# A graph-attention aggregation kernel: the sum over eight slot columns moves from VectorE to TensorE

## The chip, the cores and the metric

The program runs on one core of one Trainium2 chip. The metric is the device time of the whole program in microseconds (us), lower is better. Before the change it took 10117.94 us, the median of three runs (10090.75 to 10120.89).

## The reference, cut to what matters

A node table of 6250 rows and 256 columns goes through four layers, each added to what came before: a graph attention (8 heads of 32), a small four-expert network gated by a second attention (4 heads of 4), a graph attention (4 heads of 64), and an eight-expert network. The change touches the first and the third:

```python
e = e_left[src] + e_right[dst]
e = jnp.where(e >= 0, e, NEG_SLOPE * e)
e_max = segment_max(e, dst, num_segments=N)
e_exp = jnp.exp(e - e_max[dst])
denom = segment_sum(e_exp, dst, num_segments=N)
alpha = e_exp / (denom[dst] + EPS)
out = segment_sum(Wh[src] * alpha[:, :, None], dst, num_segments=N)
```

For each of 6250 nodes, then, the rows of all its neighbours (206250 edges with both directions and the loops) are fetched, weighed by a softmax over the neighbours, and added up. All is float32.

## The kernel before, in words

The program is a sequence of blocks. In order: a sort of the edges by node, a ranking of the nodes by degree with dense work beside it, the first large aggregation, a ranking, a small aggregation with the four small experts beside it, a ranking, the last large aggregation, a dense stage, and the experts. `aggregate` is called twice, for the first large aggregation (8 heads of 32, rows of 272 words, a sort of the next lists beside it) and for the last (4 heads of 64, rows of 264 words, nothing beside it). In the trace they lie from 1002 to 3682 us and from 6250 to 8757 us. In both, 256 columns of result per node are made.

The nodes are ranked by degree and cut into 49 tiles of 128, one node to a partition, degrees rising. A node's neighbours are slots along the free dimension, gathered by GpSimd, one indirect DMA for one slot of all 128 nodes (L914), into a ring of 96 slots (`Stream.gpsimd`). Eight slots are a unit; a tile has three to eight of them and here fits one chunk (`nk` is 1, `ng` its slots). The two aggregations each gather 1728 slots. GpSimd waits on `taken` before it fills a ring entry of 16 slots again.

For each tile (`tile(t)` on VectorE, written out 49 times in the program with a loop over chunks and one over units inside):

- ScalarE, in `lay` (L1138 to L1146), copies the score columns of the gathered slots to `el`, as soon as the tile's last slot is in (`ready`), one tile ahead of VectorE, and then counts `laid`.
- VectorE makes the scores (L1055 to L1067), ScalarE the exponentials into `prob` in PSUM (L1155).
- VectorE weighs the tile's last unit into `wide` in SBUF (`weigh`, L1042), and then for each other unit (L1075 to L1080) weighs it into `part` in PSUM and adds `part` to `wide`. Both hold 2048 columns, eight slots of 256. `taken` frees the unit's ring space.
- The end of the chunk is L1081 to L1095: the sum of the exponentials (`dsum`), the old `den` and `acc` times their scale, then the eight slots of `wide` halved to four, two and one (L1087, L1089, L1091), and `acc` plus that (L1095).
- In the first aggregation VectorE then does its share of the sort (`beside.vector`, L177 to L197): ten or eleven steps a tile in tiles 0 to 16, three or four in tiles 17 to 48. Steps "turn" and "back" are transposes on TensorE (L217, L220), copied from PSUM by ScalarE (L234, L236). TensorE does nothing else in this block.
- The end of the tile is L1100 to L1108: `den` is inverted and `res` made as `acc` times `den`; ScalarE stores it (L1127).

All waits are on semaphores that count up, against values worked out in registers of each engine from the tile's sizes (`sizes_of`, L1006). Each engine runs its own program in the order in which it is written; nothing reorders it.

## Time and profile before

| What | Value |
|---|---|
| Median of three runs | 10117.94 us (10090.75 to 10120.89) |
| Span of the profiled execution | 10110.4 us; its own time is not listed apart from the three runs |
| VectorE busy | 5594.3 us (55%), 8828 instructions |
| GpSimd busy | 5337.1 us (53%) |
| TensorE matmul busy | 2288.8 us (23%) |
| ScalarE busy | 1093.7 us (11%) |
| Gathers of L914, 4320 in three aggregations | 4275.8 us, 990 ns each |
| Weighing into `part`, L1042, x420 | 964.4 us, 2296 ns each |
| Adding `part` to `wide`, L1080, x420 | 960.4 us, 2287 ns each |

The busy shares are averages over a dozen stages. The page's chain of waits names only the very end of the program, so what bounds an aggregation has to be read from the waits and the timeline inside its own stretch. "issue" in a row is idle time for which the profile shows no wait; names ending in q are an engine's instruction sequencer.

### The profile page before, as it was taken

How to read it: one execution, taken by the hardware profiler on the slowest of the kernel's cores; microseconds unless marked ns; L12 is line 12 of the kernel's file. 1: busy time of each engine (PE TensorE's matmuls, PEld its weight loads, DVE VectorE, ACT ScalarE, POOL GpSimd, SP SyncE). 2: the span in 40 equal slices, each digit the busy share in tenths (PEclk: the TensorE clock that was granted, in tenths of full speed). 3: DMA queues.
4: the chain of work that ended last, by engine and by line, in shares of the span. 5: the costliest groups of instructions: out<-in, count | busy, mean ns of one | idle time of the engine just before them, and what ended most of it. 6: DMA issues, size and time to landing. Idle time of an engine off the chain costs nothing. (4 is left out here: it accounts for less than half of the span.)

```text
span 10110.4 us, 54577 instructions
## 1 busy us (share of the span) xinstructions
PE 2288.8 (23%) x9111; PEld 1752.0 (17%) x9112; DVE 5594.3 (55%) x8828; ACT 1093.7 (11%) x2533; POOL 5337.1 (53%) x5411
## 2 busy tenths in 40 slices
PE   2112000000000002146555512000000000129995
PEld 1111000000000001135444411000000000116663
DVE  8764588788777677523333275455656556421111
ACT  1101000000000001112222201000000000002221
POOL 0025656666676654455555345776666777542221
PEclk7555555555555555578777755555555555559997
DMA  4051333433333353411111162433333333620004
GB/s 142 22 159 50 97 82 87 122 99 98 101 101 98 102 113 74 122 23 33 29 28 28 30 172 89 109 100 92 101 98 101 106 99 99 129 97 30 30 30 117
DMA packets 458121, 869.43 MB, mean 86 GB/s; under 512 B 175134, under 2 KB 294860, under 8 KB 448192
## 3 DMA queue, kind: packets, MB, share of 16 engines
q0 software_dynamic: 239536, 575.99, 23.0%
q1 hardware_dynamic: 167648, 182.04, 6.2%
q10 hardware_dynamic: 50788, 110.02, 3.3%
q14 instruction: 129, 1.06, 0.0%
q8 instruction: 20, 0.33, 0.0%
HBM read 693.35 MB, written 180.71 MB: 86 GB/s over the span
## 5 line engine op out<-in xcount | busy, mean ns | idle before, releaser
L914 POOL DMA_INDIRECT agg_ring<-table,agg_idx x4320 | 4275.8, 990 | 2329.8 <-issue 1323.4
L1042 DVE TENSOR_TENSOR agg_part<-agg_ring,agg_prob 128x2048 f32 x420 | 964.4, 2296 | 631.8 <-issue 556.2
L1080 DVE TENSOR_TENSOR agg_wide<-agg_wide,agg_part 128x2048 f32<-128x2048 f32 x420 | 960.4, 2287 | 14.4
L1786 PE MATMUL dense_tp<-all_ident,dense_xn 128*128 128x128 f32 x100 | 23.9, 425 | 2570.3 <-issue 2543.7
L1408 PE MATMUL agg_hp<-agg_xt,agg_w 128*128 128x256 f32 x1600 | 446.4, 439 | 579.4 <-ACT agg_ht L1378 340.3
L2208 DVE TENSOR_TENSOR experts_h<-experts_sg,experts_hp 128x682 f32<-128x682 f32 x106 | 91.8, 866 | 779.7 <-ACT experts_sg L2191 779.7
L2158 PE MATMUL experts_hp<-mixture_w,experts_xt 128*128 x1696 | 518.2, 458 | 0.6 <-ACT experts_xt L2187 0.6
L1408 PEld LDWEIGHTS agg_hp<-agg_xt,agg_w 128*128 128x128 f32 x1600 | 352.4, 224 | 663.8 <-ACT agg_ht L1378 360.4
L1786 PEld LDWEIGHTS dense_tp<-all_ident,dense_xn 128*128 128x128 f32 x100 | 20.3, 228 | 2571.9 <-issue 2544.5
L2129 POOL DMA_INDIRECT yc<-experts_ysb,experts_list x105 | 103.7, 987 | 685.2 <-DVE experts_ysb L2217 685.2
L1422 PE MATMUL agg_yp<-agg_w,agg_ht 128*128 128x256 f32 x1600 | 405.3, 411 | 231.0 <-remote 174.5
L1422 PEld LDWEIGHTS agg_yp<-agg_w,agg_ht 128*128 128x128 f32 x1600 | 330.4, 208 | 297.1 <-issue 246.9
L1042 DVE TENSOR_TENSOR agg_wide<-agg_ring,agg_prob 128x2048 f32 x98 | 224.2, 2288 | 275.0 <-issue 198.8
L488 POOL IOTA rank_thresholds<- 128x50 int32 x3 | 0.5, 170 | 686.4 <-POOLq L75 686.4
L2158 PEld LDWEIGHTS experts_hp<-mixture_w,experts_xt 128*128 128x128 f32 x1696 | 314.4, 190 | 174.6 <-issue 30.0
L217 PE MATMUL agg_words_turned<-all_ident,last_sort_words 128*128 128x128 f32 x48 | 10.9, 416 | 1454.1 <-issue 1454.1
L2179 PE MATMUL experts_yp<-mixture_w,experts_ht 128*128 x1260 | 309.4, 387 | 0.0
L1155 ACT ACTIVATE agg_prob<-agg_score 128x648 f32<-128x648 f32 (+1 forms) x98 | 56.7, 579 | 2332.1 <-issue 1387.9
L1055 DVE TENSOR_TENSOR agg_score<-agg_el,agg_er 128x640 f32<-128x640 f32 (+1 forms) x98 | 64.6, 659 | 410.0 <-issue 372.4
L514 POOL DMA_INDIRECT rank_start_g<-starts,rank_node_i x147 | 143.3, 975 | 225.9 <-DVE rank_degt L625 182.0
L217 PEld LDWEIGHTS agg_words_turned<-all_ident,last_sort_words 128*128 128x128 f32 x48 | 8.8, 216 | 1456.4 <-issue 1456.0
L522 POOL DMA_INDIRECT rank_wide<-copies,rank_widx x147 | 148.9, 1013 | 195.6 <-DVE rank_widx L679 154.8
(421 smaller groups left out, 6520.8 us busy)
## 6 DMA issues: line engine op xcount, KB each, us to landing
agg_ring<-table,agg_idx POOLq DMA_INDIRECT x4320
y<-agg_ysb ACTq DMA_DIRECT2D x25, 1024.0 KB
rank_y<-y SPq DMA_DIRECT2D x10, 2560.0 KB
rank_x<-x SPq DMA_DIRECT2D x30, 640.0 KB
copies<-first_sort_words SPq DMA_DIRECT2D x16, 1024.0 KB
copies<-last_sort_words ACTq DMA_DIRECT2D x16, 1024.0 KB
x<-rank_x SPq DMA_DIRECT2D x20, 640.0 KB
agg<-agg_res ACTq DMA_DIRECT2D x98, 128.0 KB
```

Of the source, the lines that this page charges most:

```text
L514: pool.indirect_dma_start(out=start_g[:, t:t + 1], out_offset=None, in_=starts.rearrange("(n a) -> n a", a=1), in_offset=bass.IndirectOffs ...
L522: pool.indirect_dma_start(out=wide[g % 2][:, u * ROW:(u + 1) * ROW], out_offset=None, in_=copies.rearrange("c (r w) -> (c r) w", w=ROW), i ...
L914: pool.indirect_dma_start(out=self.ring[:, to:to + self.RW], out_offset=None, in_=self.table, in_offset=bass.IndirectOffsetOnAxis(ap=index ...
L1042: return dve.tensor_tensor(to[:, :].rearrange("p (j h c) -> p j h c", j=UNIT, h=H), ring[:, ds(st.at(at_u), UNIT * RW)].rearrange("p (j w) ...
L1055: dve.tensor_tensor(sc3, el3, er[:, H:2 * H].unsqueeze(1).to_broadcast([P, SC // H, H]), ALU.add).then_inc(added, 1)
L1080: dve.tensor_tensor(wide[:, :], wide[:, :], part[:, :], ALU.add).then_inc(widened, 1)
L1408: mm = pe.matmul(self.hp[:, h:h + 2 * P], self.w1[:, at:at + P], xt3[:, :, k * P:(k + 1) * P], start=(k == 0), stop=(k == 1))
L1422: mm = pe.matmul(y, self.ht[:, n * 2 * P + u * P:n * 2 * P + (u + 1) * P], self.w2[:, n * D:(n + 1) * D], start=(c == 0), stop=(c == 3))
L2129: pool.indirect_dma_start(out=yc, in_=ysb[t % B][:, :], in_offset=None, out_offset=bass.IndirectOffsetOnAxis(ap=lst[:, t * 4 + 1:t * 4 + 2 ...
L2158: mm = pe.matmul(hp3[:, c, 0:HC], xt[:, kc * P:(kc + 1) * P], rhs, start=(kc == 0), stop=(kc == 1))
L2179: mm = pe.matmul(yp[:, 0:D], ht[0:m, j * P:(j + 1) * P], w2[0:m, ds(e * W2 + j * D, D)], start=(j == 0), stop=(j == HJ - 1))
L2208: dve.tensor_tensor(h[:, :].rearrange("p (c n) -> p c n", c=2), sg[:, :].rearrange("p (c n) -> p c n", c=2), hp3[:, 2:4, 0:HC], ALU.mult). ...
```

## The change

In both large aggregations TensorE adds up the eight slots of `wide`. After a chunk's last unit has been added (`widened`), it multiplies the identity with each of the eight 256-column pieces of `wide`, all accumulating in `part[:, 0:256]` in PSUM (`folded`). VectorE no longer halves `wide` three times and has no `summed`. The folded sum is added to `acc` either before the weighing of the next chunk or tile (`merged`), while ScalarE makes the exponentials, or, for the result, into `res`, which is then multiplied by `den` in a second instruction (`completed`). TensorE now needs the tile's sizes in its registers. The sizes are stored as six 16-bit words instead of five 32-bit ones, one of them split in two.

```diff
 def aggregate(...):
-        sizes = s.sb("sizes", [1, 5 * (NT + 1)], I32)
+        sizes = s.sb("sizes", [1, LOAD * (NT + 1)], mybir.dt.uint16)
+        bits, split = s.sb("bits", [1, 2 * (NT + 1)], I32), s.sem("split")
...
-            ng, nk, c0, k0, missing = nc.values_load_multi_w_load_instructions(sizes[0:1, ds(t * 5, 5)], ...)[1]
+            ng, nk, c_high, c_low, k0, missing = nc.values_load_multi_w_load_instructions(
+                sizes[0:1, ds(t * LOAD, LOAD)], ...)[1]
...
             @block.vector
+                dve.memset(part[:, 0:CW], 0.0).then_inc(const, 1)
...
+                dve.sem_inc(folded, 1)
...
                 def tile(t):
                     ng, nk, c0, k0, _ = sizes_of(dve, t)
+                    kn = dve.snap(k0 + nk)
                     with dve.Fori(0, nk) as k:
...
                         dve.tensor_tensor(sc3, sc3, mn[:, :].unsqueeze(1).to_broadcast([P, SC // H, H]), ALU.subtract).then_inc(scored, 1)
+                        dve.wait_ge(folded, kk)
+                        dve.tensor_tensor(acc[:, :], acc[:, :], part[:, 0:CW], ALU.add).then_inc(merged, 1)
                         dve.wait_ge(probs, kk)
...
                         dve.wait_ge(tail, kk)
+                        dve.wait_ge(merged, kk)
...
                         dve.tensor_tensor(acc3, acc3, prob_scale.unsqueeze(2).to_broadcast([P, H, C]), ALU.mult).then_inc(scaled, 1)
-                        dve.wait_ge(widened, n1)
-                        dve.tensor_tensor(wide[:, 0:4 * CW], wide[:, 0:4 * CW], wide[:, 4 * CW:8 * CW], ALU.add).then_inc(quartered, 1)
-                        dve.wait_ge(quartered, kk)
-                        dve.tensor_tensor(wide[:, 0:2 * CW], wide[:, 0:2 * CW], wide[:, 2 * CW:4 * CW], ALU.add).then_inc(halved, 1)
-                        dve.wait_ge(halved, kk)
-                        dve.tensor_tensor(summed[:, :], wide[:, 0:CW], wide[:, CW:2 * CW], ALU.add).then_inc(folded, 1)
+                        dve.tensor_tensor(den[:, :], den[:, :], dsum[:, :], ALU.add).then_inc(dens, 1)
                         dve.wait_ge(scaled, kk)
-                        dve.tensor_tensor(den[:, :], den[:, :], dsum[:, :], ALU.add).then_inc(dens, 1)
-                        dve.wait_ge(folded, kk)
-                        dve.tensor_tensor(acc[:, :], acc[:, :], summed[:, :], ALU.add).then_inc(combined, 1)
...
-                    dve.tensor_tensor(res[:, :].rearrange("p (h c) -> p h c", h=H), acc3,
+                    dve.wait_ge(folded, kn + 1)
+                    dve.tensor_tensor(res[:, :], acc[:, :], part[:, 0:CW], ALU.add).then_inc(completed, 1)
+                    dve.wait_ge(completed, t + 1)
+                    res3 = res[:, :].rearrange("p (h c) -> p h c", h=H)
+                    dve.tensor_tensor(res3, res3,
                                       den[:, :].unsqueeze(2).to_broadcast([P, H, C]), ALU.mult).then_inc(tile_done, 1)
...
             @block.tensor
+                def fold(t):
+                    ng, nk, c0, _, _ = sizes_of(pe, t)
+                    with pe.Fori(0, nk) as k:
+                        gg = c0 + k * ng
+                        n1 = pe.snap((gg + ng) // UNIT + cfg.RU)
+                        pe.wait_ge(widened, n1)
+                        for j in range(UNIT):
+                            mm = pe.matmul(part[:, 0:CW], S["ident"][:, :], wide[:, j * CW:(j + 1) * CW], start=j == 0, stop=j == UNIT - 1)
+                        mm.then_inc(folded, 1)
...
+                if beside.parts:
+                    for t in range(NT):
+                        fold(t)
+                        beside.tensor(pe, t)
+                else:
+                    with pe.Fori(0, NT) as t:
+                        fold(t)
```

VectorE, end of a chunk in the first aggregation (a tile with three sort steps behind it). Before:

```order
L1081 TENSOR_REDUCE agg_dsum<-agg_prob 128x8
L1083 TENSOR_TENSOR agg_den<-agg_den,agg_prob 128x8 [waits agg0_totalled]
L1085 TENSOR_TENSOR agg_acc<-agg_acc,agg_prob 128x256 [waits agg0_shrunk]
L1086 REGISTER_ALU
L1087 TENSOR_TENSOR agg_wide<-agg_wide 128x1024 [waits agg0_widened]
L1089 TENSOR_TENSOR agg_wide<-agg_wide 128x512 [waits agg0_quartered]
L1091 TENSOR_TENSOR agg_summed<-agg_wide 128x256 [waits agg0_halved]
L1093 TENSOR_TENSOR agg_den<-agg_den,agg_dsum 128x8 [waits agg0_scaled]
L1095 TENSOR_TENSOR agg_acc<-agg_acc,agg_summed 128x256 [waits agg0_folded]
L1049 REGISTER_ALU [waits agg0_combined,agg0_dens]
L1049 COMPARE_AND_BRANCH
L197 TENSOR_TENSOR last_sort_words<-last_sort_words 128x2x64x4 [waits last_sort_words_compared]
```

And with the change:

```order
L1097 TENSOR_REDUCE agg_dsum<-agg_prob 128x8
L1099 TENSOR_TENSOR agg_den<-agg_den,agg_prob 128x8 [waits agg0_totalled]
L1101 TENSOR_TENSOR agg_acc<-agg_acc,agg_prob 128x256 [waits agg0_shrunk]
L1102 TENSOR_TENSOR agg_den<-agg_den,agg_dsum 128x8
L1062 REGISTER_ALU [waits agg0_scaled,agg0_dens]
L1062 COMPARE_AND_BRANCH
L197 TENSOR_TENSOR last_sort_words<-last_sort_words 128x2x64x4 [waits last_sort_words_compared]
```

Five instructions fewer lie between the last unit and the sort (or, in the last aggregation, the end of the tile). At the end of the same tile one instruction of before, L1108, has become two, with a wait for TensorE (`folded`) and the register instruction of that wait ahead of them:

```order
L1107 MEMSET agg_m 128x8
L1109 TENSOR_SCALAR agg_den<-agg_den 128x8 [waits agg0_reset]
L1111 RECIPROCAL agg_den<-agg_den 128x8 [waits agg0_floored]
L1115 ISA [waits agg0_out_stored,agg0_inverted]
L1116 TENSOR_TENSOR agg_res<-agg_acc,agg_part 128x256 [waits agg0_folded]
L1119 TENSOR_TENSOR agg_res<-agg_res,agg_den 128x256 [waits agg0_completed]
```

TensorE, sort transposes of tiles 13 (L217, a turn) and 14 (L220, the way back). Before:

```order
L217 MATMUL agg_words_turned<-all_ident,next_sort_words 128x128 [waits next_sort_words_copied,next_sort_words_compared]
L217 MATMUL agg_words_turned<-all_ident,next_sort_words 128x128 x7
L220 MATMUL agg_words_turned<-all_ident,next_sort_words 128x128 [waits next_sort_words_copied,next_sort_words_compared]
L220 MATMUL agg_words_turned<-all_ident,next_sort_words 128x128 x7
L217 MATMUL agg_words_turned<-all_ident,next_sort_words 128x128 [waits next_sort_words_copied,next_sort_words_compared]
```

And with the change:

```order
L217 MATMUL agg_words_turned<-all_ident,next_sort_words 128x128 [waits next_sort_words_copied,next_sort_words_compared]
L217 MATMUL agg_words_turned<-all_ident,next_sort_words 128x128 x7
L1011 TENSOR_LOAD agg_sizes
L1129 UNCONDITIONAL_BRANCH
L1129 ISA
L1134 MATMUL agg_part<-agg_wide,all_ident 128x256 [waits agg0_widened]
L1134 MATMUL agg_part<-agg_wide,all_ident 128x256 x7
L1129 REGISTER_ALU
L1129 COMPARE_AND_BRANCH
L220 MATMUL agg_words_turned<-all_ident,next_sort_words 128x128 [waits next_sort_words_copied,next_sort_words_compared]
L220 MATMUL agg_words_turned<-all_ident,next_sort_words 128x128 x7
L1011 TENSOR_LOAD agg_sizes
```

The way back of tile 14 was next in line on TensorE once VectorE had compared; now the fold of tile 14, which waits for that tile's last unit, stands between the two.

## Rows read from the trace of the kernel before

**Rows 1.** busy time by stretch: from, to, us, each engine busy (instructions), PEclk, DMA share, GB/s

```profile
1002.00:3682.00 2680.00, 49.97 (x208) 39.87 (x208) 2008.21 (x2144) 178.63 (x457) 1720.85 (x1729) 0.50 0.37 97
6250.00:8757.00 2507.00, 0.00 (x0) 0.00 (x0) 1440.70 (x1445) 116.18 (x414) 1767.46 (x1763) 0.50 0.38 97
```

**Rows 2.** groups of VectorE, 1000 to 3680 us: shapes, count, busy us, mean ns, idle before

```profile
L1080 DVE TENSOR_TENSOR agg_wide<-agg_wide,agg_part 128x2048 f32<-128x2048 f32 x210 | 480.2, 2287 | 7.2
...
L1087 DVE TENSOR_TENSOR agg_wide<-agg_wide 128x1024 f32<-128x1024 f32 x49 | 59.9, 1222 | 0.0
...
L1108 DVE TENSOR_TENSOR agg_res<-agg_acc,agg_den 128x256 f32<-128x256 f32 x49 | 21.5, 439 | 14.7 <-DVE agg_den L1104 6.0 <-remote 3.8 <-issue 3.6
```

**Rows 3.** why GpSimd's gathers (L914) waited, 1000 to 3670 us (us, times)

```profile
  DVE agg_part L1042: 384.7, 35
```

**Rows 4.** the same, 6300 to 8770 us

```profile
  DVE agg_part L1042: 146.2, 28
```

**Rows 5.** timeline, scores laid out (ACT) and taken up (DVE): start us, us, [idle before]

```profile
1086.92 0.74 ACT L1146 ACTIVATE agg_el<-agg_negs 128x640 f32 x1 [1.09 <-issue]
...
1132.52 0.82 DVE L1055 TENSOR_TENSOR agg_score<-agg_el,agg_er 128x640 f32<-128x640 f32 x1 [1.03 <-issue]
...
3387.46 0.74 ACT L1146 ACTIVATE agg_el<-agg_negs 128x640 f32 x1 [1.09 <-issue]
...
3390.80 0.83 DVE L1055 TENSOR_TENSOR agg_score<-agg_el,agg_er 128x640 f32<-128x640 f32 x1 [1.02 <-issue]
...
3617.12 0.83 DVE L1055 TENSOR_TENSOR agg_score<-agg_el,agg_er 128x640 f32<-128x640 f32 x1 [27.63 <-ACT agg_el L1146]
...
8488.40 0.49 DVE L1055 TENSOR_TENSOR agg_score<-agg_el,agg_er 128x320 f32<-128x320 f32 x1 [7.12 <-issue]
```

**Rows 6.** timeline of VectorE, end of one tile of the first aggregation

```profile
2119.16 0.82 DVE L1081 TENSOR_REDUCE agg_dsum<-agg_prob 128x8 f32<-128x640 f32 x1
...
2120.21 0.42 DVE L1085 TENSOR_TENSOR agg_acc<-agg_acc,agg_prob 128x256 f32<-128x256 f32 x1
...
2122.53 0.43 DVE L1091 TENSOR_TENSOR agg_summed<-agg_wide 128x256 f32<-128x256 f32 x1
2122.87 0.22 DVE L1093 TENSOR_TENSOR agg_den<-agg_den,agg_dsum 128x8 f32<-128x8 f32 x1
...
2123.77 0.69 DVE L197 TENSOR_TENSOR last_sort_words<-last_sort_words 128x512 f32<-128x512 f32 x1 [0.35 <-DVE agg_acc L1095]
```

**Rows 7.** timeline of VectorE, end of one tile of the last aggregation

```profile
7497.41 2.29 DVE L1080 TENSOR_TENSOR agg_wide<-agg_wide,agg_part 128x2048 f32<-128x2048 f32 x1
...
7504.88 0.43 DVE L1108 TENSOR_TENSOR agg_res<-agg_acc,agg_den 128x256 f32<-128x256 f32 x1 [0.49 <-issue]
7509.78 0.49 DVE L1055 TENSOR_TENSOR agg_score<-agg_el,agg_er 128x320 f32<-128x320 f32 x1 [4.47 <-issue]
```

**Rows 8.** timeline of TensorE: 128x256 matmuls after work, after idling, one by one

```profile
4297.90 1.89 PE L1408 MATMUL agg_hp<-agg_xt,agg_w 128*128 128x256 f32 x8
4309.23 3.78 PE L1408 MATMUL agg_hp<-agg_xt,agg_w 128*128 128x256 f32 x8 [9.44 <-issue]
...
4315.35 0.38 PE L1422 MATMUL agg_yp<-agg_w,agg_ht 128*128 128x256 f32 x1 [1.92 <-issue]
```

**Rows 9.** timeline of TensorE and ScalarE, one turn of the sort

```profile
1384.40 1.97 PE L217 MATMUL agg_words_turned<-all_ident,next_sort_words 128*128 128x128 f32 x8 [439.17 <-DVE next_sort_words L190]
...
1386.40 0.60 ACT L234 ACTIVATE next_sort_words<-agg_words_turned 128x512 f32<-128x512 f32 x1 [0.26 <-issue]
```

**Rows 10.** timeline of VectorE, first weighing of a tile behind the exponential

```profile
3620.78 0.83 DVE L1067 TENSOR_TENSOR agg_score<-agg_score,agg_mn 128x640 f32<-128x640 f32 x1
3623.13 2.29 DVE L1042 TENSOR_TENSOR agg_wide<-agg_ring,agg_prob 128x2048 f32 x1 [1.52 <-ACT agg_prob L1155]
```

**Rows 11.** register instructions at L1042, first then last aggregation: ns min/median/max

```profile
L1042 DVEq FUSED_REGOPS  x567: 4/168/1425, 1062.6 to 3656.4; - x189
...
L1042 DVEq FUSED_REGOPS  x567: 4/698/1414, 6365.6 to 8742.1; - x189
```

35 lines of the change are left out of this document (20 added, 15 removed).

## The prediction

> **What bounds the kernel now.** The page's chain names only the end of the program, so I read the two aggregations by stretch. [rows 1] is the first view: over 2680 us and 2507 us VectorE is busy 75% and 57%, GpSimd 64% and 71%, TensorE hardly or not at all, with its clock at 0.50. Neither engine fills its stretch, so the next view is who waits for whom. GpSimd's gathers wait for VectorE to free ring space for 384.7 us in the first aggregation [rows 3] and 146.2 us in the last [rows 4]. Third comes the other direction. VectorE begins a tile at L1055; what it needs from the gathers is there when L1146 ends. I looked at all 98 such pairs. In the first aggregation the scores of tile 1 lie ready 45 us before they are taken up, those of tile 45 still 2.6 us (3387.46 + 0.74 to 3390.80), and only the last tile, 48, waits for them, 27.6 us [rows 5]. So VectorE sets the pace of tiles 1 to 47, with the reserve shrinking as the tiles grow. In the last aggregation tiles 0 to 7 begin as soon as their scores are ready (gathers bind), tiles 8 to 37 have 6 to 35 us of reserve (VectorE binds), and after tile 37 GpSimd gathers with hardly a wait until the last tile, so that its own pace counts; tile 45 begins late again [rows 5]. So about 30 of 49 tiles there are paced by VectorE.
>
> **First aggregation, end of a chunk.** From L1081 to the sort's first step the row times give 2123.77 - 2119.16 = 4.61 us [rows 6]. With the change the three halvings and the last addition go. L1085 still ends 1.47 us after L1081 began; the addition to `den` follows as closely as it does behind L1091 (0.34 us after its start), lasts 0.16 to 0.22 us, and the loop's branch costs 0.35 us as now: 1.95 us. That takes off 2.66 us.
>
> **End of the tile.** L1108 (0.44 us, [rows 2]) becomes two instructions of that size, 0.42 us plus 0.03 between: +0.45 us. The one more register instruction is 0.05 us, or 0.7 us where such instructions are slow [rows 11]; some seven tiles of this stretch are so (their unit loops are longer than those of tiles with as many units), +5 us. Net 2.2 us a tile. `part` lies in PSUM. A 2048-column addition that reads PSUM takes 2287 ns, a 1024-column one in SBUF 1222 ns [rows 2]; the difference is 1065 ns, 1.04 ns for each further column, and between that SBUF one and a 512-column step of the sort in SBUF (0.69 us, [rows 6]) it is also 1.04 ns a column. So I charge nothing for PSUM. The Trainium skill, "VectorE: DVE Perf Modes", in the section on the errata, gives a PSUM source 62 cycles more of fixed time than an SBUF one. By it the 98 additions into `res` would cost some 6 us more, an estimate from that page; the trace does not bear it out.
>
> **The merge** into `acc` (0.42 us) stands between L1067 and the wait for the exponentials. VectorE idles 1.52 us there [rows 10], 0.71 us of it for ScalarE: it is covered, at nothing; uncovered it would be 0.42 us x 98 = 41 us.
>
> **The fold.** Eight 128x256 float32 matmuls took 1.89 us behind other work and 3.78 us after 9 us of idling [rows 8]. TensorE idles for some 30 us before nearly every fold, and [rows 1] has its clock at 0.50 throughout, 1.2 GHz; I take 3.8 us, plus 0.1 us for semaphores each way: ready 4.0 us after the last unit. The Trainium skill, "TensorE: Matmul & The Clock Gate", in the section on what is happening, calls the throttled clock the default and says that activity releases it; the rows agree, with 1.89 and 3.78 us. Were the clock at its upper level here, the fold would take 1.9 us and the last aggregation save about 1.5 us a tile more, 45 us in all. In the first aggregation VectorE has at least 5 us of sort between, so nobody waits for the fold.
>
> **Transposes behind the fold.** In tiles 10, 14 and 16 (and 37) the sort's first step is a turn or a way back that TensorE now does before the tile's end, and then behind its fold. There VectorE would be ready 1.95 us after L1081 starts, but fold (3.9), eight transposes (1.97) and the last copy (0.26 + 0.60) [rows 9] end at 6.7 us: 4.8 us lost in each, and about 8 us in tile 37, with sixteen transposes. Together 22 us. In the other sixteen, sort work of VectorE lies ahead of the transpose.
>
> **Sum of the first.** 48 tiles x 2.2 = 106 us; minus 22 for the transposes and 5 for slow register instructions; minus 4 because tiles 44 and 45 have too little reserve to run 7 us ahead of the gathers [rows 5]; minus 2 for tile 47, whose gain is lost in the last tile's wait: 73 us.
>
> **Sum of the last.** Here nothing lies between chunk and tile end. Before, L1108 ends at 7505.31, 5.6 us after the last L1080 (7497.41 + 2.29 = 7499.70) [rows 7]. With the change the fold is ready at +4.0; then 0.42, 0.03 and 0.42: +4.9. VectorE arrives at about +3.2, so it stands 0.8 us for TensorE. Gain 0.7 us (0.3 where register instructions are quick). x 30 tiles = 21 us, and 0.7 for the last tile. The other 18 are paced by the gathers and gain nothing. `lay` on ScalarE and the loads of six sizes have the reserve above them; the constants at the start cost about 1 us twice.
>
> 73 + 22 - 2 = 93 us. The profiled span is 10110.4 us, 7.5 us below the median of the runs; 10110.4 - 93 = 10017 as a span, and 10025 as a median. By the bounds: without the losses to transposes and reserve 120 us; with a PSUM read that costs 6 us in all after all, half the merge uncovered and a fold of 4.5 us, 93 - 6 - 20 - 15 = 52 us. So the forecast's own range is 9998 to 10066.
>
> **Rivals.**
> *TensorE issues slowly, and VectorE stands for it (slower).* New code on TensorE once ran one matmul at a time, 1.92 us idle before one of 0.38 us [rows 8]. A fold at 2.3 us a matmul is 18 us. In the last aggregation each VectorE-paced tile stands 14 us longer, 30 x 14 = 420 us; in the first the sort hides 8 to 16 us of it, another 6 us a tile, 290 us: some 10700 us. It decides from a fold of 4.0 + 93/30 = 7 us. Against it: all 20 turns and ways back in the first aggregation, also written out once each, ran without gaps [rows 9]. 10%.
> *The gathers bind (no change).* GpSimd's 384.7 us of waits are unevenly spread, and the reserve of VectorE falls to 2.6 us at tile 45. If the ring of 96 slots passes on only a part, and the fold eats the last aggregation's 21 us, 25 us are left: 10093 us. 12%.
> *Register instructions change their pace (either sign).* At L1042 they last 168 ns in the first and 698 ns in the last aggregation, the same 567 of them [rows 11]: same code, and the trace does not say what makes them slow. The change moves all code. If the slow kind spreads over the first, up to 567 x 0.53 = 300 us more, some 10320 us; a third of it eats the gain. 7%. If it leaves the last, VectorE gains as much, but GpSimd has only 146 us of waits to give, of which 20 are spent above: 9900 us. 8%.
>
> **How the numbers follow.** The forecast has 63%, the rivals 10, 12, 7 and 8%. What can be told from no change is 0.3%, 30 us: 10088 to 10148. Faster: 63 + 8 + 2 (a mild form of the second rival) = 73%. Slower: the first and the bad half of the third, 17%. The same: 10%. The range goes from 9900 (the good half of the third) to 10125 (the second rival with a margin); what lies above is left out, some 17%.
>
> **What would show it.** L1087 to L1095 gone; the start of the sort about 2.0 us after the start of the `dsum` reduction; folds of 3.8 us at a clock of 0.50; no wait for the fold in the first aggregation but one of 5 us for ScalarE's copies in tiles 10, 14 and 16; in the last a wait of 0.8 us on TensorE ahead of the addition into `res`; the first aggregation 70 us and the last 20 us shorter, with GpSimd's waits down by about as much. Wrong it would be if GpSimd's waits fell and the stretches did not (gathers bind), if folds took over 7 us, or if the median of the register instructions moved in either stretch.

## The result, and the profile after

The changed kernel takes 10385.79 us (median of five runs, 10383.11 to 10399.96) where the kernel before takes 10117.94: a ratio of 1.0266, 95% interval 1.025 to 1.0283. The forecast was 10025, faster; the time lies far above the range. The profiled execution spans 10381.2 us, 270.8 more than before. A sum of the stretches, from a stretch's first gather to its last result, says where: the first aggregation takes 2886.7 us and not 2664.3 (+222.4), the last 2456.6 and not 2434.0 (+22.6), the small aggregation and the rankings between them 25.0 more, the rest 0.8. The code between the two is unchanged, and over the traces of the experiments from chips like this one the small aggregation takes 1490 to 1561 us (1518 before, 1537 after), so the 25.0 us are not shown to come from the change.

The page of the profile after: each engine's busy time, then TensorE's busy share and its granted clock in 40 slices, in tenths.

```profile
PE 2858.1 (28%) x10679; PEld 2188.5 (21%) x10680; DVE 5411.3 (52%) x8638; ACT 1093.1 (11%) x2533; POOL 5254.5 (51%) x5411
...
PE   2212011111111111225654432011111111129995
...
PEclk9555555555555555557877765555555555559997
```

VectorE is busy 183 us less, as the change meant it to be, and the program is longer. The same two stretches as [rows 1], in the same columns:

```profile
1002.00:3905.00 2903.00, 327.75 (x992) 252.27 (x992) 1915.26 (x2049) 178.24 (x457) 1708.11 (x1728) 0.55 0.35 90
...
6555.00:9027.00 2472.00, 293.98 (x784) 224.46 (x784) 1343.37 (x1316) 111.97 (x405) 1662.57 (x1729) 0.55 0.38 98
```

x784 for 49 folds is 16 records a fold, not eight. I come back to that.

VectorE's groups in the last aggregation, in the columns of [rows 2]. What is new is the idle time ahead of L1116, the addition that takes the fold into `res`; what has gone is idle time ahead of the weighing (L1054, L1042 before) and of the scores (L1068, L1055 before).

```profile
L1054 DVE TENSOR_TENSOR agg_part<-agg_ring,agg_prob 128x2048 f32 x210 | 482.3, 2297 | 109.3 <-issue 51.4 <-DVE agg_wide L1096 44.8 <-DVE agg_wide L1054 13.1
...
L1068 DVE TENSOR_TENSOR agg_score<-agg_el,agg_er 128x320 f32<-128x320 f32 x49 | 24.3, 497 | 136.9 <-issue 136.9
...
L1116 DVE TENSOR_TENSOR agg_res<-agg_acc,agg_part 128x256 f32<-128x256 f32 x49 | 20.7, 422 | 776.1 <-remote 583.8 <-issue 188.0 <-PE agg_part L1134 4.3
```

The kernel before, same groups in its last aggregation:

```profile
L1042 DVE TENSOR_TENSOR agg_part<-agg_ring,agg_prob 128x2048 f32 x210 | 482.2, 2296 | 491.5 <-issue 480.9 <-DVE agg_wide L1080 5.4 <-DVE agg_wide L1042 5.2
...
L1055 DVE TENSOR_TENSOR agg_score<-agg_el,agg_er 128x320 f32<-128x320 f32 x49 | 24.1, 492 | 293.1 <-issue 283.1 <-ACT agg_el L1146 6.5 <-DMA agg<-agg_res 3.5
```

So the fold costs 776 us of standing, 15.8 us a tile, and the stretch is only 23 us longer, because some 640 us of other idle time went (382 ahead of the weighing into `part`, 104 ahead of that into `wide`, and 156 ahead of the scores), and 97 us of additions. With the first two go slow register instructions: at L1054 they have the quick pace in both stretches now, against [rows 11] (first, then last aggregation).

```profile
L1054 DVEq FUSED_REGOPS  x567: 46/211/306, 1063.4 to 3881.7; - x189
...
L1054 DVEq FUSED_REGOPS  x567: 46/211/701, 6613.7 to 9010.6; - x189
```

One tile end of the last aggregation (TensorE, then VectorE), the place of [rows 7]:

```profile
7443.09 5.35 PE L1134 MATMUL agg_part<-agg_wide,all_ident 128*128 128x256 f32 x16 [42.89 <-DVE agg_wide L1096]
...
7444.89 0.18 DVE L1111 RECIPROCAL agg_den<-agg_den 128x4 f32<-128x4 f32 x1
7455.73 0.42 DVE L1116 TENSOR_TENSOR agg_res<-agg_acc,agg_part 128x256 f32<-128x256 f32 x1 [10.66 <-remote]
```

TensorE begins 0.05 us after the last addition to `wide`, all 16 records are issued within 5.0 us, and VectorE gets the sum 12.6 us after the first. "remote" means that the profile has no instruction that ends when the wait does: as recorded, the matmuls ended long before. Over the 49 tiles that time is 10 to 21 us, 19 in the middle, with one exception, the last tile, when no gather is under way any more and no further TensorE instruction comes behind the fold. There it is 6.2 us:

```profile
9014.98 6.16 PE L1134 MATMUL agg_part<-agg_wide,all_ident 128*128 128x256 f32 x16 [82.17 <-DVE agg_wide L1096]
...
9021.18 0.42 DVE L1116 TENSOR_TENSOR agg_res<-agg_acc,agg_part 128x256 f32<-128x256 f32 x1 [4.32 <-PE agg_part L1134]
```

In the first aggregation the stands for the fold are 170 us in 26 tiles, but the larger part is elsewhere. TensorE and then ScalarE, a turn of the sort behind a fold:

```profile
3065.85 6.01 PE L1134 MATMUL agg_part<-agg_wide,all_ident 128*128 128x256 f32 x16 [44.40 <-issue]
3071.70 1.04 PE L217 MATMUL agg_words_turned<-all_ident,last_sort_words 128*128 128x128 f32 x8
3096.11 1.12 PE L217 MATMUL agg_words_turned<-all_ident,last_sort_words 128*128 128x128 f32 x4 [23.38 <-issue]
...
3095.46 0.60 ACT L234 ACTIVATE last_sort_words<-agg_words_turned 128x512 f32<-128x512 f32 x1 [43.40 <-remote]
3104.56 0.60 ACT L234 ACTIVATE last_sort_words<-agg_words_turned 128x512 f32<-128x512 f32 x1 [8.50 <-remote]
```

The x8 are two groups of four transposes. A free TensorE gives the first group to ScalarE 1.2 us after its start; here it comes 23.8 us after it, and the second group 32.9. VectorE's idle time ahead of its sort steps (L184, L190, L197) rises from 179 to 407 us, GpSimd's waits for VectorE from 384.7 [rows 3] to 634.6 us, those of [rows 4] from 146.2 to 252.7.

### The profile page after: what moved, and what is told of

Same layout as the page of the kernel before. It is cut to its first block and busy times, and to the rows that moved or that the text cites. A ratio compares the mean times of both kernels' runs of the same rounds, so it can differ in the third digit from the quotient of the medians.

```text
span 10381.2 us, 58165 instructions
## 1 busy us (share of the span) xinstructions
PE 2858.1 (28%) x10679; PEld 2188.5 (21%) x10680; DVE 5411.3 (52%) x8638; ACT 1093.1 (11%) x2533; POOL 5254.5 (51%) x5411
## 5 line engine op out<-in xcount | busy, mean ns | idle before, releaser
L914 POOL DMA_INDIRECT agg_ring<-table,agg_idx x4320 | 4192.4, 970 | 2679.7 <-issue 1298.0
L1134 PE MATMUL agg_part<-agg_wide,all_ident 128*128 128x256 f32 x1568 | 583.2, 552 | 4637.0 <-DVE agg_wide L1096 2651.0
L1134 PEld LDWEIGHTS agg_part<-agg_wide,all_ident 128*128 128x128 f32 x1568 | 446.0, 292 | 4773.7 <-DVE agg_wide L1096 2672.5
L1054 DVE TENSOR_TENSOR agg_part<-agg_ring,agg_prob 128x2048 f32 x420 | 964.6, 2297 | 219.7 <-DVE agg_wide L1096 104.2
L1116 DVE TENSOR_TENSOR agg_res<-agg_acc,agg_part 128x256 f32<-128x256 f32 x98 | 41.3, 422 | 950.7 <-remote 729.4
L1054 DVE TENSOR_TENSOR agg_wide<-agg_ring,agg_prob 128x2048 f32 x98 | 224.2, 2288 | 153.0 <-ACT agg_prob L1183 83.6
L190 DVE TENSOR_TENSOR last_sort_words<-last_sort_words 128x1024 f32<-128x1024 f32 x176 | 209.3, 1230 | 91.7 <-ACT last_sort_words L236 64.2
L506 POOL DMA_INDIRECT rank_row<-words,rank_qi x150 | 152.0, 1013 | 193.0 <-DVE rank_junk L593 89.9
```

What stands on the lines that cost most here:

```text
L190: dve.tensor_tensor(b[:, :, half, :], a[:, :, 0, :], a[:, :, 1, :], op).then_inc(self.cmp_done, 1)
L506: pool.indirect_dma_start(out=row[i % 2][:, v * COARSE:(v + 1) * COARSE], out_offset=None, in_=rows, in_offset=bass.IndirectOffsetOnAxis(a ...
L914: pool.indirect_dma_start(out=self.ring[:, to:to + self.RW], out_offset=None, in_=self.table, in_offset=bass.IndirectOffsetOnAxis(ap=index ...
L1054: return dve.tensor_tensor(to[:, :].rearrange("p (j h c) -> p j h c", j=UNIT, h=H), ring[:, ds(st.at(at_u), UNIT * RW)].rearrange("p (j w) ...
L1134: mm = pe.matmul(part[:, 0:CW], S["ident"][:, :], wide[:, j * CW:(j + 1) * CW], start=j == 0, stop=j == UNIT - 1)
```

## The experiments

The changed kernel's aggregations are the base of all edits. The experiments ran on seven chips, and these are of two kinds. On four, like the one above, the kernel before takes 10089 to 10122 us; on three it takes 9118 to 9128 us. Each comparison of times below is with the kernel before on the same chip; traces of the kernel before exist from the first chip alone. e1, e2, e6, f3 and g3 ran once each, so their totals carry no interval.

The theory at the start: beside the gathers each matmul of a fold arrives late. Its rivals: a fixed hold of the last signal, and a burst after which TensorE is slow.

**How many matmuls (e1_count, e6_count_again).** VectorE halves `wide` 0, 0, 1, 2 or 3 times, TensorE folds the rest, the first class twice over.

```diff
+                    count = (16, 8, 4, 2, 1)[t % 5]
...
+                        for again in range(2 if count == 16 else 1):
+                            n = min(count, UNIT)
+                            for j in range(n):
```

> The changed kernel, but the number of 128x256 matmuls in a fold goes round with the tile: 16 (the eight done twice), 8, 4, 2, 1; VectorE halves `wide` zero, zero, one, two or three times before, so the result stays right. In the changed kernel the eight leave TensorE's records within 6 us but are taken up by VectorE 12 to 21 us after the first one's start (last aggregation). Theory 'each is slow beside the gathers' (about 1.2 us for each of the 16 records): in the last aggregation the time from a fold's first matmul to the addition into res is about 38, 19, 10, 5 and 2.5 us. Rival 'a fixed hold' (what is late is only the signal of the last one): about 19 us for every number. Rival 'a burst switches TensorE down' (slow only after some 3 us of unbroken work, when the granted clock steps): 2 and 1 matmuls arrive in under 2.5 us, 4 in 4 to 6, 8 in 19, 16 in much more than 30.

It ran on a chip where before takes 9119.42 us: 9139.59. From first matmul to the addition into `res`, in the last aggregation, in the middle: 9.7, 5.8, 3.8, 2.1 and 1.3 us. Nothing is late there, gathers or not, and all three theories were left without a case; so it went to another chip.

> e1_count once more, on another chip. On a chip where before takes some 10120 us (as in e5) and a fold of eight is taken up 12 to 21 us after its first matmul, the numbers 16, 8, 4, 2, 1 tell what the lateness is. 'Each matmul is late' (about 2.4 us for each of the eight): 38, 19, 10, 5, 2.5 us. 'A fixed hold of the last signal': 26, 19, 17, 15, 14 us. 'A burst of over some 3 us switches TensorE down': 16 and 8 late, 4 at most 4 us, 2 and 1 at 2.1 and 1.3 us. On a chip where before takes 9119 us: 9.7, 6.0, 3.8, 2.1, 1.3 us, as in e1_count.

Before 10122.06, this 10571.3 us. In the same order now: 24 to 64 us for sixteen (43 in the middle), 9 to 19 us for eight (17), and 3.6 to 3.8 us for four, in all ten tiles. Two and one were there when VectorE came for them or within 2.4 us. Three tiles in a row, TensorE and VectorE:

```profile
8375.92 9.27 PE L1147 MATMUL agg_part<-agg_wide,all_ident 128*128 128x256 f32 x32 [54.28 <-issue]
...
8427.51 0.42 DVE L1125 TENSOR_TENSOR agg_res<-agg_acc,agg_part 128x256 f32<-128x256 f32 x1 [47.83 <-remote]
...
8463.11 6.58 PE L1147 MATMUL agg_part<-agg_wide,all_ident 128*128 128x256 f32 x16 [77.92 <-issue]
...
8481.46 0.42 DVE L1125 TENSOR_TENSOR agg_res<-agg_acc,agg_part 128x256 f32<-128x256 f32 x1 [17.54 <-issue]
...
8513.56 3.54 PE L1147 MATMUL agg_part<-agg_wide,all_ident 128*128 128x256 f32 x8 [43.87 <-issue]
...
8517.14 0.42 DVE L1125 TENSOR_TENSOR agg_res<-agg_acc,agg_part 128x256 f32<-128x256 f32 x1 [2.63 <-issue]
```

Four matmuls leave x8 records of 3.54 us; eight leave x16. The lateness is neither the same for each matmul nor a fixed hold of the signal: four matmuls are on time, the excess for eight is some 12 us and for sixteen some 33. That kills the first two theories as they were stated.

**No gathers (e2_no_gathers).** Ten more folds behind the last tile of each aggregation, each after ten VectorE instructions on `wide`.

```diff
+                for i in range(10):
+                    pe.wait_ge(again, i + 1)
+                    for j in range(UNIT):
+                        mm = pe.matmul(part[:, CW:2 * CW], S["ident"][:, :], wide[:, j * CW:(j + 1) * CW], start=j == 0, stop=j == UNIT - 1)
+                    mm.then_inc(refolded, 1)
```

> The changed kernel with ten more folds of eight matmuls behind the last tile of each aggregation, each after ten VectorE instructions of about 2.3 us on `wide`, when no gather is under way; VectorE waits for each. Theory 'slow beside the gathers': each of these is there about 6 us after its first matmul, as the last tile's own (6.2 us). Rival 'a burst switches TensorE down': 12 to 20 us each, like the folds inside the aggregation, whatever the gathers do. Rival 'fixed hold by what follows on TensorE': between them. The rest of the kernel as the changed one; the total about 2 x 10 x (24 + 6) = 600 us more.

9645.59 us, before 9119.42: a chip without lateness, so it told nothing of the gathers' part; the added folds arrive after 5.2 to 6.8 us, the ordinary ones of the last aggregation after 5.1 to 6.8. It was not repeated on a chip of the other kind, so whether gathers must be under way for the lateness is open. What speaks for it is the last tile of the last aggregation, whose fold arrives after 6.1 to 6.5 us in all four traces of the change from chips with late folds.

**Nobody stands for the fold (e3_deferred, e7_deferred_again; e4_deferred_swapped, e8_swapped_again).** `wide`, `acc` and `den` alternate by tile, the sum has a PSUM bank of its own (the sort's transposes give up one), and VectorE takes it at the end of the next chunk; e4 and e8 also put the transposes ahead of the fold.

```diff
+                        dve.wait_ge(folded, kk1)
+                        dve.tensor_tensor(accs[:, ds(whose, CW)], accs[:, ds(whose, CW)], total, ALU.add).then_inc(merged, 1)
...
-                        fold(t)
-                        beside.tensor(pe, t)
+                        beside.tensor(pe, t)
+                        fold(t, wides[t % 2])
```

> TensorE's fold stays, but nobody stands for it: `wide`, `acc` and `den` alternate between two buffers by tile, the sum goes to a PSUM bank of its own, VectorE takes it into the tile's `acc` at the end of the next chunk (0.42 us) and makes the result then, ScalarE stores it one tile later. If the stand for the fold is the cause of the loss in the last aggregation (584 us there by the waits), the last aggregation is no longer than before the change (2434 us from first gather to last result, or some 20 to 60 us less), and what remains is the loss of the first, where turns of the sort stand behind the fold: some 150 to 250 us slower than before there, total 10150 to 10300 us. If something else costs the time (register instructions, the loads of sizes), the total stays near 10390.

> As e3_deferred, and TensorE does the tile's transposes of the sort before the tile's fold instead of behind it. If the turns were late only because they stood behind a slow fold, the first aggregation is as long as before the change or up to 100 us shorter (48 tiles x 2.2 us), total 9950 to 10100 us. If the fold leaves TensorE slow for tens of us, whatever the order, turns stay late and the total is near e3_deferred's.

Where before takes 9119.42 us: 9067.35 (ratio 0.9944, 0.9927 to 0.996) and 9054.92 (0.9931, 0.9915 to 0.9948).

> e3_deferred once more, on another chip. Where signals of TensorE are late (before 10120 us): nobody stands for the fold, so by the waits shown in the changed kernel the last aggregation loses 770 us of stands against it and is bound by the gathers again or by VectorE; total 10000 to 10200 us. Rival 'the sort's late turns are most of the loss': 10250 us and more. Where before takes 9119 us: 9067 us as in e3_deferred.

> e4_deferred_swapped once more, on another chip. Where signals of TensorE are late: if the turns of the sort are late only because they stand behind the fold, 100 to 200 us less than e7_deferred_again; if TensorE stays slow for tens of us after a fold, or turns are late by themselves, within 50 us of it. Where before takes 9119 us: 9055 us as in e4_deferred_swapped.

Where before takes 10122.06 us: 10450.6 (1.0335, 1.0311 to 1.0359), worse than the change itself, and 10165.12 (1.0048, 1.0033 to 1.0063). The time expected for e7, 10000 to 10200 us, missed, and its rival, that late turns are most of the loss, came out: nobody stands for the fold, and the first aggregation still takes 2945 us (2896 in the change on the same chip, e9), because the turns stand behind it. The order alone makes 270 us of that: in e8, which differs from e7 in nothing else, the same stretch takes 2675 us, VectorE idles 205 us ahead of sort steps and not 448, and the total is 285 us less, where 100 to 200 were expected. So on these chips late turns are the main loss of the first aggregation. The lateness passes: in e8 ScalarE's first copy of most turns comes 1.15 us after the turn begins. Not told apart in e7 and e8 is what the lost bank costs, with which each group of four transposes waits for the copy of the one before.

The stand itself cost the last aggregation next to nothing. It takes 2461 us in e7 and 2459 in e8, where nobody stands, and 2455 in e9 with 774 us of stands, on the same chip. Without the stands the register instructions at L1054 are slow again there, 690 ns in the middle in both.

**The change on each kind of chip (e5_after_again, e9_after_third, g1_after_fourth, h2_after_fifth).** No edit.

> The changed kernel itself, unedited, beside the kernel before on the chip of the experiments, where before takes 9119 us and not 10118. In the four experiments there a fold of eight arrives 5.4 to 6.8 us after its first matmul (last tile of the recorded profile: 6.2), with and without gathers. Theory 'the time depends on how late TensorE's signals arrive on a chip': here the addition into res in the last aggregation waits about 4 us and not 16, no turn of the sort is late, and the verdict turns: by the terms of the prediction with a fold of 6 us instead of 3.8, first aggregation 70 us shorter, last 0 to 40 us longer, total 9050 to 9120 us, ratio 0.992 to 1.000. Rival 'the change costs 2.7% on any chip': 9360 us.

> The changed kernel itself beside these on the same chip. 10380 us and a ratio of 1.025 where before takes 10120 us; where before takes 9119 us and a fold arrives 6 us after its first matmul, 9050 to 9120 us and a ratio of 0.992 to 1.000 (as expected for e5_after_again, which ran on a chip of the first kind).

> The changed kernel, unedited, once more. So far it ran only on chips where before takes 10120 us (ratio 1.025 and 1.027). Where before takes 9120 us: e2_no_gathers had the changed kernel's first aggregation in 2411 us and the last in 2196 us from first gather to last result, against 2400 and 2196 in e4_deferred_swapped at 9055 us in all; so 9055 to 9085 us, a ratio of 0.993 to 0.996. Where before takes 10120: 1.026 again.

> The changed kernel, unedited, on the same chip as h1_split. Where before takes 9120 us: from e2_no_gathers, whose time less its twenty extra folds (292 and 290 us, by the same stretches in e3_deferred) is 9062 us, 9055 to 9085 us, a ratio of 0.993 to 0.996. Where before takes 10120 us: 1.022 to 1.027 again.

The first three fell on chips of the first kind: 10371.6 against 10121.78 (1.0254, 1.024 to 1.0268), 10388.46 against 10122.06 (1.0272, 1.0246 to 1.0297), 10302.42 against 10097.05 (1.0216, 1.0192 to 1.0239). The last did not: 9067.64 us against 9118.5, a ratio of 0.9946, 0.9929 to 0.9962. There the change is faster, by 0.5%. Its stretches in the columns of [rows 1]:

```profile
975.00:3402.00 2427.00, 328.44 (x992) 253.39 (x992) 1917.08 (x2049) 175.05 (x457) 1724.08 (x1728) 0.55 0.42 107
...
5522.00:7732.00 2210.00, 290.21 (x784) 221.92 (x784) 1342.64 (x1315) 108.31 (x405) 1644.28 (x1728) 0.56 0.43 109
```

And what VectorE and GpSimd waited for there, in the last aggregation:

```profile
DVE agg_score L1068 <- ACT agg_el L1174: 441.0, 37, 47.3
DVE agg_res L1116 <- PE agg_part L1134: 199.4, 49, 4.8
...
POOL agg_ring L914 <- DVE agg_part L1054: 8.2, 9, 5.8
```

The same busy times to within 1.5% (ScalarE's within 3.5%), and from first gather to last result the first aggregation is 475 us shorter than in the changed kernel's first trace, the last 262. The fold costs 4.1 us of standing a tile, GpSimd waits for VectorE 8.2 us in all, and VectorE waits for scores of slots just gathered: here the gathers set the pace of the last aggregation.

**Short folds throughout (f1_half, g2_half_again; f2_half_deferred).** One halving stays on VectorE, TensorE folds four; f2 is this with nobody standing.

```diff
+                        dve.wait_ge(widened, n1)
+                        dve.tensor_tensor(wide[:, 0:4 * CW], wide[:, 0:4 * CW], wide[:, 4 * CW:8 * CW], ALU.add).then_inc(halved, 1)
...
-                        for j in range(UNIT):
+                        for j in range(UNIT // 2):
```

> The change with shorter folds: VectorE adds the two halves of `wide` once (1.22 us, right behind the unit loop) and TensorE folds four pieces, in about 3.8 us, as the folds of four in the runs before. If what loses time on a chip with late folds is TensorE's work beyond some 3.8 us in one go, the wait ahead of the addition into res falls from 16 to 3 us, no turn of the sort is late, first aggregation 30 to 50 us shorter than before the change, last within 40 us: total 10070 to 10140 us (where before takes 10120), 9060 to 9120 us (where before takes 9119). If every TensorE result is late beside VectorE's wait, 10300 us and more.

> Folds of four as in f1_half, and nobody stands for them (two buffers of `wide`, `acc`, `den`, result made one tile later, transposes ahead of the fold, as in e8_swapped_again). VectorE gives up 1.1 us of additions a tile against before in both aggregations. If bursts are the cause, 10030 to 10110 us where before takes 10120 (e8_swapped_again: 10165), so this one beats the kernel before; where before takes 9119 us, within 20 us of e4_deferred_swapped's 9055. If the deferral itself costs (more register instructions, of the slow kind), it stays near 10160.

> f1_half once more, for a chip with late folds. Where before takes 10120 us: burst theory 10070 to 10140 us, wait ahead of the addition into res 3 us, no late turns, first aggregation (first gather to last result) 2620 to 2670 us against 2664 before and 2887 in the changed kernel; rival 'every TensorE result is late there' 10300 and more. Where before takes 9128: 9147 as in f1_half.

Where before takes 9128.34 us: 9147.31 (1.0022, 1.0012 to 1.0031) and 9148.87 (1.0022, 1.0012 to 1.0032). Both missed: f1 lies 27 us above its range and f2 94 us above the 9055 that it should have been near; f2 was not run on the other kind. On such a chip the 1.22 us of the halving is paid in the first aggregation, which takes 2460 us in f1 and 2414 with the fold of eight in f3 on the same chip. Where before takes 10097.05: 10170.78 (1.0076, 1.0059 to 1.0093), above what I expected. The stand ahead of the addition into `res` is at most 3.0 us (108 us for 48 tiles) and the last aggregation 2436 us, as before the change, but the first takes 2741 us, and VectorE's idle time ahead of sort steps is still 279 us. As I read it, a turn right behind a fold of four is too much work again; no run tests that. And the slow register instructions of the last aggregation are back.

```profile
L1054 DVEq FUSED_REGOPS  x567: 3/697/1395, 6400.4 to 8776.9; - x189
```

**A pause in the fold (f3_pause, g3_pause_again).** In the last aggregation alone the fold is done four and four, and VectorE zeroes unused columns 6 or 12 times between.

```diff
+                            if j == UNIT // 2 - 1 and not beside.parts:
+                                mm.then_inc(halfway, 1)
+                                pe.wait_ge(go, pe.snap(k0 + k + 1))
```

> The change's fold of eight, in the last aggregation alone done as four and four, with a pause between: VectorE waits for the first four, then writes zeros into unused columns of `part` 6 or 12 times (0.95 us each, odd and even tiles), then lets TensorE go on; result unchanged. If the unbroken burst is the cause, on a chip with late folds each half arrives 3.8 us after its first matmul. If it is the volume (eight matmuls within some time), the second half arrives as late as in the changed kernel, 8 to 15 us after its own first matmul, above all behind the short pause. First aggregation as the changed kernel's (2890 us from first gather to last result).

> f3_pause once more, for a chip with late folds: burst theory, each half 3.8 us after its first matmul whatever the pause; volume rival, second half 8 to 15 us after its own first matmul behind the short pause (6 instructions) and less behind the long one (12). Where before takes 9128 us: 3.8 us in any case, as in f3_pause.

f3 (9355.08 us, before 9128.34): 3.8 us for each half. g3 (10450.02 us, before 10097.05): the first half is in VectorE's hands after at most 4.2 us in all 49 tiles; the second after at most 3.82 us in all 25 tiles with the long pause, and after 3.5 to 9.4 us (7.3 in the middle) with the short one, over 4 us in 16 of 24. Two tiles, the long pause and the short, TensorE and then VectorE:

```profile
8467.69 3.78 PE L1141 MATMUL agg_part<-agg_wide,all_ident 128*128 128x256 f32 x8 [39.11 <-issue]
8486.10 3.68 PE L1141 MATMUL agg_part<-agg_wide,all_ident 128*128 128x256 f32 x8 [14.62 <-issue]
8524.30 3.78 PE L1141 MATMUL agg_part<-agg_wide,all_ident 128*128 128x256 f32 x8 [34.53 <-issue]
8535.50 3.78 PE L1141 MATMUL agg_part<-agg_wide,all_ident 128*128 128x256 f32 x8 [7.42 <-issue]
...
8489.81 0.42 DVE L1123 TENSOR_TENSOR agg_res<-agg_acc,agg_part 128x256 f32<-128x256 f32 x1 [3.83 <-issue]
...
8544.91 0.42 DVE L1123 TENSOR_TENSOR agg_res<-agg_acc,agg_part 128x256 f32<-128x256 f32 x1 [9.52 <-remote]
```

So it is no matter of an unbroken run alone: behind the short pause the first half still counts in 16 of 24 tiles, behind the long one in none. Within these stretches that fits a limit on what TensorE has lately done, from which it recovers when left alone. It is not shown that TensorE's load alone decides, and the last section has a stretch that speaks against it.

**The fold cut in two, deferred (h1_split, h3_split_again).** e4 with the second four begun when the next tile's first unit is added. This is right as long as a tile is one chunk, as here.

```diff
+                            if j == UNIT // 2 and pause:
+                                pe.wait_ge(widened, n2)
```

> e8_swapped_again's kernel with the fold of eight cut in four and four: TensorE goes on with the second four when VectorE has added the first unit of the next tile's chunk (some 15 us after the first four began; this form is right where every tile is one chunk, as with these inputs). Burst theory: no part of the fold is late on any chip and no turn of the sort stands behind one. Where before takes 10120 us: 10080 to 10160 us (e8: 10165), and whether it beats before hangs on the register instructions of 0.7 us in the last aggregation, of which this form has some more. Where before takes 9120 us: 9055 us as e4_deferred_swapped, a ratio of 0.993.

> h1_split once more, for a chip with late folds. Where before takes 10120 us: burst theory 10080 to 10160 us, every half of a fold there within 4 us, no late turns; e8_swapped_again, whose fold is unbroken, took 10165. If it is no less than e8, the rest of the loss is VectorE's own (register instructions of 0.7 us), not TensorE's lateness. Where before takes 9120 us: 9052 us again.

9052.37 us against 9118.5 (0.993, 0.9913 to 0.9946), and 10110.93 against 10089.29 (1.002, 1.0007 to 1.0032). On the late chips that is 0.3% better than e8 by the ratios, whose intervals just do not meet, and the fold loses nothing that I can find: the first aggregation takes 2644.5 us against 2664.3 in the trace before (on another chip of the kind), and VectorE's idle time ahead of sort steps is 186 us against 179. What is left does not look like the fold. The last aggregation takes 2450.7 us against 2434.0. VectorE's idle time on "issue" there is 408 us ahead of the weighing into `part` (481 before), but 210 ahead of that into `wide` (140), 128 ahead of the product into `res` (15) and 55 ahead of taking in the fold, and its register instructions have the slow pace:

```profile
L1054 DVEq FUSED_REGOPS  x567: 2/691/1396, 6373.8 to 8764.0; - x189
```

This form is level with e4 where nothing is late and the best edit where folds are late, but there it does not beat the kernel before.

## Why the prediction was wrong

- **The step that failed is "The fold", and with it "Sum of the last" and "Transposes behind the fold".** It read [rows 8] as eight matmuls in 3.78 us. A row's x counts records, and a float32 matmul of this kernel leaves two (a transpose one): four matmuls are x8 in 3.54 us, eight are x16. Even with nothing late a fold takes 6.0 us in the middle, not 3.8. The page before could have told: the loops of L1408 issue 32 matmuls for each of 25 blocks, 800 in all, and it counts 1600.

```profile
L1408 PE MATMUL agg_hp<-agg_xt,agg_w 128*128 128x256 f32 x1600 | 446.4, 439 | 579.4 <-ACT agg_ht L1378 340.3
```

  The Trainium skill, "FP8 and Floating Point Precision", in the section on TensorE's precision, gives true float32 four passes through the array; the trace agrees, with two records of 0.44 us for each 256 columns, some 0.22 us four times.
- **On the chip of the result it then took 19 us in the middle, and VectorE stood 15.8 us a tile for it, not 0.8.** The forecast took a result to be there when its records end. The first aggregation before already had rows against that, and the "ran without gaps" of the first rival looked at records alone. The sixteen transposes of one turn lie within 3.38 us, and ScalarE, which copies four at a time, gets the third group 9.1 us after the start and the fourth 20.3 (TensorE, then those two copies of ScalarE). On a chip without lateness (h2) the four copies of such a run follow at 1.2, 2.0, 3.0 and 3.7 us.

```profile
3160.42 3.38 PE L217 MATMUL agg_words_turned<-all_ident,last_sort_words 128*128 128x128 f32 x16 [183.58 <-issue]
...
3169.49 0.60 ACT L234 ACTIVATE last_sort_words<-agg_words_turned 128x512 f32<-128x512 f32 x1 [6.47 <-remote]
3180.75 0.60 ACT L234 ACTIVATE last_sort_words<-agg_words_turned 128x512 f32<-128x512 f32 x1 [10.66 <-remote]
```

- **VectorE came for the fold some 2 us after its first matmul and not 3.2** (12.64 less 10.66 us in the tile shown above), at the quick pace of the register instructions. On a chip without lateness a fold of 6.0 us therefore costs 4.1 us of standing.
- **The sign stood larger in a stretch of which I read TensorE's rows alone [rows 8].** In the small aggregation, where TensorE works in long runs, ScalarE and VectorE waited for it without a recorded cause. From the kernel before (4255 to 5774 us), and then from the changed kernel on a chip without lateness (3940 to 5040 us):

```profile
ACT agg_ht L1378 <- remote: 504.0, 46, 32.2
...
DVE agg_ysb L1394 <- remote: 170.5, 15, 32.7
```

```profile
ACT agg_ht L1406 <- PE agg_hp L1436: 226.3, 106, 4.3
```

  The longest such wait is 32 us on the one and 4.3 us on the other, for the same matmuls. The stretch takes 1518 us on the first and 1084 on the second.
- **Rival "TensorE issues slowly, and VectorE stands for it" was the right outcome by the wrong mechanism.** It priced a fold at 18 us, as it came, and said 10700 us. The issue was in time, what came late was the result. And it charged the stand in full: it left out that VectorE's register instructions turn quick when VectorE stands, some 490 us of idle time in the last aggregation. Its 10% was too little.
- **Transposes:** 22 us for four tiles became 228 us more of idle time ahead of sort steps, 107 of it in those four tiles and 121 in others, whose transposes were called covered. They were taken as late by the fold's length; TensorE stays late after it.
- **What held:** the sort begins 1.85 us after L1097 (2115.70 against 2113.85; forecast 1.95). L1082 is hidden behind ScalarE's exponential, as forecast: idle time ahead of the first weighing falls from 120.4 to 102.3 us. `part` in PSUM costs the additions nothing: L1116 takes 422 ns and L1082 414, the SBUF additions L1091 and L1095 425 each. So the 62 cycles of the Trainium skill, "VectorE: DVE Perf Modes", section on the errata, are not borne out here. L1116 and L1119 are 0.42, 0.03 and 0.42 us.
- **Where results are not late the change gains 50.9 us,** just under the forecast's smallest gain, 52. That it comes so near is in part luck: the stand is 4.1 us and not 0.8, and goes unseen because the gathers set the pace of the last aggregation there (the second rival). That the first aggregation gives all of the gain follows from this but is not shown, since no trace of the kernel before was taken on such a chip.
- **Register instructions:** the last aggregation got the quick pace, which the third rival priced at 9900 us. It came with stands, so that it gave back and did not give.

## What to carry to other kernels

Before work is moved to an engine that idles, read how it behaves under load of that length, in whatever stretch of the trace has it: in these traces waits for it marked "remote" meant that its results came later than its records ended. Look for the sign in the stretch to be changed above all: the stage with TensorE's longest runs here shows no such wait (last section), the aggregation does. Check how many records one instruction leaves before a row's x is used as a count. Keep added work short and off the waits of others, put it behind what has a reader, and compare on more than one chip: here one change is 2.2 to 2.7% slower on some and 0.5% faster on others.

## What was not expected of the hardware

- **Chips differ by 10% for the same kernel**: 9118 to 9128 us on three, 10089 to 10122 us on four and on the first. The first aggregation of the changed kernel takes 2411 us on the one kind, 2852 to 2906 on the other. Two things mark the slower ones, late matmuls and register instructions of 0.7 us; on the others neither appears (at L1054 the longest takes 0.31 us). Why, and whether the two have one cause, no run tells.
- **The granted clock does not tell of the lateness.** One late fold of the changed kernel, in four pieces (TensorE and weight loads, VectorE, ScalarE, GpSimd busy, then PEclk):

```profile
7443.00:7446.40 3.40, 3.31 (x8) 2.69 (x9) 1.60 (x8) 0.00 (x0) 2.51 (x3) 0.50 0.44 119
7446.40:7449.80 3.40, 2.03 (x10) 1.45 (x8) 0.00 (x0) 0.00 (x0) 2.76 (x3) 1.00 0.41 108
7449.80:7453.20 3.40, 0.00 (x0) 0.00 (x0) 0.00 (x0) 0.00 (x0) 2.48 (x4) 1.00 0.35 98
7453.20:7456.60 3.40, 0.00 (x0) 0.00 (x0) 0.84 (x2) 0.00 (x0) 2.48 (x4) 0.51 0.41 119
```

  It is at 1.2 GHz in the first piece and at 2.4 in the next two, and in the third nothing is recorded any more, while the result is still out; on the chips without lateness the clock rises in a fold as well. In g3 three second halves came after 7.9, 8.1 and 9.4 us with no rise in or between the halves. The forecast took 1.2 GHz throughout, the smaller of its errors. The Trainium skill, "TensorE: Matmul & The Clock Gate", in the section on seeing it yourself, warns that the trace's clock events have been found unreliable; no run here shows that they are wrong, only that they do not separate late from timely.
- **In the last aggregation on late chips VectorE's register instructions are slow unless VectorE stands for long at each tile's end**: 211 ns in the middle with stands of 16 us, 690 to 698 with 3 us or none (before, e7, e8, g2, h3). Not explained.
- **TensorE's load alone does not make it late.** In the stage with the eight experts of the kernel before, on the first chip, TensorE works for 800 us without a gap, and nobody waits for a late result. The stretch, in the columns of [rows 1], and ScalarE's longest kind of wait for TensorE in it:

```profile
9100.00:9900.00 800.00, 800.00 (x3333) 550.70 (x3332) 125.58 (x186) 183.28 (x371) 180.55 (x185) 1.00 0.10 30
...
ACT experts_sg L2191 <- PE experts_hp L2158: 365.4, 93, 3.9
```

  The changed kernel on a chip without lateness has the same wait 93 times, 365.3 us, at most 3.9. None of the 2122 register instructions behind 9100 us takes over 0.2 us. So both marks of the slower chips are missing there, on such a chip. Among what that stage lacks is the gathering of slots into the ring (the DMA share is 0.35 to 0.43 in the rows of the aggregations above and 0.10 in it); no run tests whether that is the cause.
